# Second attention of a two-layer program: mask and row maximum in one VectorE instruction

## The reference, cut to what matters

```python
keys    = einsum('bse,neh->bsnh', residual, W_key) + Bias_key
queries = einsum('bse,neh->bsnh', residual, W_query) + Bias_query
values  = einsum('bse,neh->bsnh', residual, W_values) + Bias_values
scores  = einsum('bknh,bqnh->bnqk', keys, queries) / sqrt(64)
scores  = where(q_idx < k_idx, 1e-10, scores)      # causal: the future gets 1e-10, not -inf
probs   = softmax(scores, axis=3)
out     = einsum('bqnh,nhe->bqe', einsum('bnqk,bknh->bqnh', probs, values), W_output) + Bias_output
```

## Time and profile before

| | |
|---|---|
| median of 3 runs | 2212.29 us (2203.16 to 2216.28) |
| profiled execution, first to last instruction | 2208.8 us |
| PE busy | 1973.9 us, 89% |
| DVE busy | 1437.3 us, 65% |
| ACT busy | 981.3 us, 44% |
| POOL busy | 585.7 us, 27% |
| second attention, batch 0 | about 686 to 1030 us |
| second attention, batch 1 | about 1770 to 2110 us |

### The profile page before, as it was taken

How to read it: one execution, slowest core, us unless ns; L and a number is a source line. 1 busy time by engine, 2 the same in 40 slices (tenths; PEclk the granted TensorE clock), 3 DMA queues, 4 the chain that set the end, 5 groups by cost and what they waited for, 6 DMA issues and landing times.

```text
span 2208.8 us, 32078 instructions
## 1 busy us (share of the span) xinstructions
PE 1973.9 (89%) x10106; PEld 1173.6 (53%) x10106; DVE 1437.3 (65%) x2492; ACT 981.3 (44%) x1377; POOL 585.7 (27%) x549
## 2 busy tenths in 40 slices
PE   6899999996997999998888999999979889999985
PEld 4444444443784555556644444444448755555554
DVE  7677788865327777753467877778561377777343
ACT  2445454441224666662334444444413256656422
POOL 0000000000101798884120000000010047897821
PEclk7999999998887999998879999999979879999987
DMA  2366665578000000000516566656760000000024
GB/s 94 84 154 160 155 147 139 141 160 236 27 1 10 3 9 6 1 1 30 162 39 153 142 145 142 144 141 152 180 199 1 1 10 11 1 6 1 1 81 134
DMA packets 84847, 188.01 MB, mean 85 GB/s; under 512 B 17697, under 2 KB 46754, under 8 KB 83106
## 3 DMA queue, kind: packets, MB, share of 16 engines
q1 hardware_dynamic: 83650, 183.76, 32.9%
q0 software_dynamic: 1024, 2.10, 0.3%
HBM read 178.47 MB, written 8.91 MB: 85 GB/s over the span
## 4 chain that ended last, share of the span: by engine, by line
PE 67%; DVE 14%; issue 9%; ACT 3%; DMA 3%; POOL 3%; SPq 1%; DVEq 0%; another core or an unknown queue 0%; POOLq 0%; ACTq 0%
PE PS L814 10%; PE PS L786 5%; PE PS L750 5%; PE PS L986 4%; PE PS L926 4%; PE PS L966 3%; DVE mx L1919 3%; PE PS L881 3%; PE PS L1159 3%; PE PS L969 3%; PE PS L771 3%; PE PS L776 3%; PE PS L1218 2%; DMA V<-weight_rows 2%; POOL Esum L2463 2%
## 5 line engine op out<-in xcount | busy, mean ns | idle before, releaser
L1919 DVE TENSOR_REDUCE mx<-PS 128x8 f32<-128x512 f32 x512 | 329.5, 685 | 178.7 <-PE PS L750 163.9
L2463 POOL TENSOR_TENSOR Esum<-Esum,EE 128x512 f32<-128x512 f32 (+3 forms) x320 | 340.2, 1092 | 15.2 <-POOL Esum L2463 10.7
L1948 DVE TENSOR_TENSOR EE<-EE,V 128x1024 f32<-128x1024 f32 x256 | 303.0, 1218 | 46.2 <-DMA V<-weight_rows 45.8
L1502 ACT ACTIVATE EE<-PS 128x1024 f32<-128x1024 f32 x256 | 260.1, 1025 | 142.5 <-PE PS L776 140.5
L2052 DVE TENSOR_REDUCE mrow<-PS 128x1 f32<-128x512 f32 (+3 forms) x384 | 204.8, 552 | 98.5 <-PE PS L929 70.3
L2405 POOL TENSOR_TENSOR QA<-hT,QA 128x512 fp32r<-128x512 f32 x2 | 2.6, 1284 | 996.8 <-ACT hT L1690 996.8
L814 PE MATMUL PS<-EE,Vlater 128*64 128x512 f32 x1024 | 250.7, 609 | 9.4 <-ACT U L1468 8.3
L750 PE MATMUL PS<-KA,QA 128*128 128x512 f32 x512 | 204.1, 454 | 31.9 <-DVE mx L1919 25.9
L1586 ACT ACTIVATE EE<-PS 128x1024 f32<-128x1024 f32 (+2 forms) x192 | 138.2, 740 | 120.2 <-PE PS L969 118.1
L771 PE MATMUL PS<-QA,KA 128*128 128x512 f32 x512 | 185.1, 443 | 0.0
L750 PEld LDWEIGHTS PS<-KA,QA 128*128 128x128 f32 x512 | 97.8, 196 | 130.5 <-DVE mx L1919 88.5
(11 more groups left out here) (321 smaller groups left out, 3386.1 us busy)
## 6 DMA issues: line engine op xcount, KB each, us to landing
V<-weight_rows SPq DMA_DIRECT2D x512, 256.0 KB, 5.5
EE<-in_w SPq DMA_DIRECT2D x48, 192.0 KB, 2.7
V<-in_Wg SPq DMA_DIRECT2D x4, 1024.0 KB, 6.4
EE<-in_Wu SPq DMA_DIRECT2D x4, 1024.0 KB, 11.4
EE<-in_Wd SPq DMA_DIRECT2D x4, 1024.0 KB, 13.2
sorted_out<-U SPq DMA_DIRECT2D x12, 256.0 KB, 3.3
wo<-in_wo SPq DMA_DIRECT2D x5, 512.0 KB, 4.4
wq_s<-in_wq SPq DMA_DIRECT2D x17, 128.0 KB, 3.0
```

The lines of the kernel that those rows point to most:

```text
L1502: act.activation(EE[i % 2][:, t, :], banks(2 * (t % 2)), ACT.Exp, scale=QSCALE).then_inc(s["p2_exp"], 1)
L1919: dve.tensor_reduce(mx[:, t, half * 8:half * 8 + 8], banks(5 + x % 2, BANK).rearrange("p (c k) -> p c k", c=8), AX, ALU.max).then_inc(s["p ...
L1948: dve.tensor_tensor(EE[i % 2][:, t, :], EE[i % 2][:, t, :], weight_ring[a % 2][:, odd, :], ALU.mult).then_inc(p3_mul, 1)
L2463: ins = pool.tensor_tensor(Esum[:, h, lo:hi], Esum[:, h, lo:hi], e_tile(t)[:, h, lo - t * P:hi - t * P], ALU.add)
```

## The change

DVE's reduction of a unit becomes a `tensor_tensor_reduce`: it adds a bf16 mask operand to the PSUM columns, writes the sum to a scratch tile (`seT`), and takes the maximum of the row and of a starting value that is read per partition. For an own unit the mask is a slice of a new tile `causal` (512 zeros, then `neg`) that ends in `neg`; for the others it is 512 zeros. The starting value is the floor `eps_row` in the first half, and the first half's maximum (`mhalf1`) in the second, so that the own unit's result goes straight into `mx1`. PE's mask product goes, and so do `top` and the semaphores `m_both` and `m_top`; `turn_maxima` waits for `mx_red` instead. A semaphore increment (`s_held`) stands between each unit's wait and its instruction.

```diff
-        ident_b = sb("ident_b", [P, P], BF16)
-        neg_b = sb("neg_b", [P, P], BF16)
+        causal = sb("causal", [P, BANK + P], BF16)
...
-        mrow1 = sb("mrow1", [P, 2, NT, 2])
-        mtop1 = sb("mtop1", [P, 2, NT])
+        mhalf1 = sb("mhalf1", [P, 2, NT // 2])
...
@@ PE, maxima
-                        own = hi == (t + 1) * P
-                        mm = pe.matmul(banks(4 + h, hi - lo), M1[h][p % 2][:, t * P:(t + 1) * P],
-                                       S1[h][p % 2][:, lo:hi], start=True, stop=not own)
-                        if own:
-                            mm = pe.matmul(banks(4 + h, P, hi - lo - P), ident_b[:, :], neg_b[:, :],
-                                           start=False, stop=True)
-                        mm.then_inc(s["mx_full"], 1)
+                        pe.matmul(banks(4 + h, hi - lo), M1[h][p % 2][:, t * P:(t + 1) * P],
+                                  S1[h][p % 2][:, lo:hi], start=True, stop=True).then_inc(s["mx_full"], 1)
...
@@ PE, turn_maxima
-                    pe.wait_ge(s["m_top"], n0 + p + 1)
+                    pe.wait_ge(s["mx_red"], (n0 + p + 1) * NU)
...
@@ PE, in front of project_qk(p + 2, 1) and project_qk(1, 1)
-                        pe.wait_ge(s["mx_red"], (n + 2) * NU)
-                pe.wait_ge(s["mx_red"], (n0 + 1) * NU)
...
@@ DVE, maxima
+                        own = (t + 1) * P == half * BANK + width
+                        floor = const("eps_row")[:, t:t + 1]
+                        if half:
+                            floor = mhalf1[:, h, t - NT // 2:t - NT // 2 + 1]
                         dve.wait_ge(s["mx_full"], n * NU + x + 1)
-                        dve.tensor_reduce(mrow1[:, h, t, half:half + 1], banks(4 + h, width), AX,
-                                          ALU.max).then_inc(s["mx_red"], 1)
-
-                def top(p):
-                    n = n0 + p
-                    dve.wait_ge(s["mx_red"], (n + 1) * NU)
-                    dve.tensor_reduce(mtop1[:, :, :], mrow1[:, :, :, :], AX, ALU.max).then_inc(s["m_both"], 1)
-                    dve.wait_ge(s["m_both"], n + 1)
-                    dve.tensor_tensor(mx1[:, :, 0:33:32].rearrange("p t h -> p h t"), mtop1[:, :, :], const("eps_row").unsqueeze(1).to_broadcast([P, 2, NT]),
-                                      ALU.max).then_inc(s["m_top"], 1)
+                        dve.sem_inc(s_held, 1)
+                        mask = causal[:, BANK + P - width:BANK + P] if own else causal[:, 0:BANK]
+                        dve.tensor_tensor_reduce(seT[:, h * BANK:h * BANK + width], banks(4 + h, width), mask, 1.0, floor, ALU.add, ALU.max,
+                                                 mx1[:, t, 32 * h:32 * h + 1] if own else
+                                                 mhalf1[:, h, t - NT // 2:t - NT // 2 + 1]).then_inc(s["mx_red"], 1)
...
@@ DVE, pair and the opening
-                        top(p + 1)
-                top(0)
...
@@ DVE, once at the start
-            dve.memset(mrow1[:, :, :, :], -3e38)
+            dve.memset(causal[:, 0:BANK], 0.0)
-            dve.tensor_copy(ident_b[:, :], ident)
-            dve.tensor_copy(neg_b[:, :], const("neg"))
+            dve.tensor_copy(causal[:, BANK:BANK + P], const("neg"))
```

More of the change, by code:

```diff
@@ L350, in layer_program @@
                                                 "mt_ps m_rows p2_full p2_exp u_full u_out").split()})
-        S[1].update({n: sem(f"{n}_1") for n in ("proj_qk hi_out lo_out proj_v v_out mx_full mx_red m_both m_top mt_ps "
+        S[1].update({n: sem(f"{n}_1") for n in ("proj_qk hi_out lo_out proj_v v_out mx_full mx_red  mt_ps "
                                                 "m_row_a m_row_b f_ps f_exp p2_full p2_exp diag val_done masked later "
@@ L2131, in pair @@
                     if follows:
-                        top(p + 1)
-                    if follows:
                         row_a(p + 1)
```

## The result

| | before | after |
|---|---|---|
| median of 4 runs each, taken together | 2209.81 us (2203.16 to 2216.28) | 2231.72 us (2229.82 to 2240.26) |
| ratio | | 1.0113 (95%: 1.0092 to 1.0134) |
| profiled execution, span | 2208.8 us | 2227.7 us |
| both second attentions, from their start to that of the experts | 723.8 us | 747.9 us |

The change costs 1.1%, 21.9 us. The forecast was 2208.0, with 2231 as its upper end.

What follows compares the result with a forecast made beforehand. Steady pairs were taken as PE-bound from unit 2 to 18, then DVE-bound until the transposes. At d = 0.12, twelve turns gave -6.7 us and two openings +2.4: 2212.3 - 4.3 = 2208.0 us, full range 2192 to 2231.

Steps and rivals of the forecast that it cites:

- step 1: Pair's start, units 0 and 1 to unit 2's product: mask -0.07, lag +0.10, plus d; together +0.03 + d us.
- step 3: From unit 8 to unit 18: five mask products gone from PE, -0.35 us; DVE's start on unit 18 moves -0.40 + 3d.
- lag: Increment between wait and instruction starts DVE +0.10 us later wherever it waits for PE, nothing where busy; ends 0 and 0.10.
- steps 1 and 2: Pair's start to unit 8: masks save PE 0.07 by unit 2, 0.28 by unit 5; unit 8 shifts -0.15 + 3d us.
- d: Time the fused instruction adds per unit on DVE: 0.12 us, with ends 0.06 and 0.25.
- Step 5: Pair's end, between unit 23's reduction and PE's transposes: `top` gone, -1.24 us a turn.
- Steps 4 and 5: Pair's end: units 18 to 23 on a busy DVE add 6d; then `top` gone gives -1.24 us.
- The opening: Start of a batch, PE and DVE alternating on two banks: 13d - 0.34, +1.2 us per batch at d = 0.12.
- DVE as the bound: Rival: at units 18 to 23, d = 0.25 costs 1.5 us against `top`'s 1.24; about 2225 us, chance 0.20.
- A free maximum: Rival: d up to 0.08, DVE's last stretch hardly grows and `top` is won in full; about 2200 us, chance 0.26.
- POOL holding up the fused instruction: Rival: each unit suffers 0.5 us beside busy POOL, d = 0.62; about 2262 us, chance 0.06.
- Freed PE time arriving: Rival: the hold-up at unit 8 dissolves, a pair shrinking by at most 2.11 us; 2187 us, chance 0.05.

Runs made afterwards that it cites:

- a_fill: Kernel after plus ten products nobody reads in PE's two waits at a pair's start (six before unit 0, four between units 1 and 2): 2210.42 us, ratio 1.0006.
- b_no_mask: Kernel before without PE's mask products, maxima taken over unmasked blocks: 2207.61 us, ratio 1.0001.
- b_no_top: Kernel before without `top`, the own unit's maximum going straight to the transposes: 2200.50 us, ratio 0.9963.
- b_fused_only: Kernel before with the fused instruction (mask of zeros) and its increment in place of the reduction, mask products and `top` kept: 2216.19 us, ratio 1.0041.
- a_fill_late: Kernel after plus ten filling products in mid-pair before the value projection, in six pairs of a batch: 2250.11 us, ratio 1.0194.
- a_early: Kernel after with unit 0 taken ahead of the wait for the second head's queries: 2204.75 us, ratio 0.9978.
- b_early: Kernel before with unit 0 taken ahead of the wait for the second head's queries, nothing else changed: 2194.30 us, ratio 0.9943.

## Why the prediction was wrong

**The step that failed** is in no term of the sum: "From unit 2 to unit 18 the chain runs through PE, product after product" was costed with PE's products as long as before. Every step held the granted clock at 1.00 and took unit 0's place behind the turn as fixed. Both moved. Unit 0 came 0.6 us later, the hop to unit 2 grew by step 1's own +0.15, and the clock fell in six of the ten turns in which it had stood at 1.00. Those six falls cost 12.7 us against the kernel's own turns without one; a_fill, with nothing changed but the waits filled, gains 21 us by the medians, first turns and last pairs included. The forecast looked at PE's wait at the end of a pair and valued it in time only.

Not every wait of that size does it. Before's own turn has PE idle for 1.15 us with the clock at 1.00, as this slice of before shows (columns as in the earlier trace rows):

```profile
822.00:824.00 2.00, 1.01 (x9) 1.04 (x10) 0.89 (x1) 0.16 (x1) 2.00 (x2) 1.00 0.00 0
```

The Trainium skill (TensorE: Matmul & The Clock Gate, A second HAM failure mode: psum-queue depth-cycling) says that an engine which idles briefly and often between groups of products can swing between its two clock levels. The runs agree: no wait of PE between the turn at 778.2 and the fall at 786.1 is over 0.86 us, and filling the waits ends the falls in the second to sixth turns.

**Point by point, at full clock.** Turn 2 of batch 0 is the clean place: the clock holds there in all the kernels of the table, and unit 0 starts 7.17 to 7.18 behind the turn.

| per turn, us | forecast | turn 2 | steady turn | from |
|---|---|---|---|---|
| mask products gone (step 3) | -0.35 | -0.34 | -0.35 | b_no_mask |
| `top` gone | -1.24 | -1.17 | -0.75 | b_no_top |
| fused instruction and lag, with the masks of steps 1 and 2 | +1.03 (9d - 0.05) | +0.41 net | +0.38 net | b_fused_only |
| all of it | -0.56 | -0.55 | +0.05 | after |

- The sum. In turn 2 it came out, -0.55 against -0.56. In a steady turn unit 0 is 0.62 later (7.91 against 7.29) and the turn 0.60 worse than in turn 2. So even with the clock at 1.00 throughout, the forecast's 6.7 us over twelve turns would have been about nothing; a_fill, whose clock holds, is level with before.
- That agreement in turn 2 is in part luck. The last `diagonal` of that pair took 0.57 (at 774.87) instead of 1.20, a gain that stands in no step. If all of it came through, the fused instructions cost about 0.6 more than the 1.03 forecast; b_fused_only, taken with its own relief, says 1.25. For the same reason the three parts of turn 2 don't add up to the whole: each meets POOL in other places.
- Masks (steps 2 and 3): right in size.
- d = 0.12: measured 0.14 where somebody waits, 0.07 on a busy DVE. The read of the accumulator is a second instruction, as the Trainium skill (VectorE: DVE Perf Modes, Two Vector instructions with no wait between them) says; 384 reads of 82 ns agree. That it runs beside the next instruction was not in the forecast.
- The lag: the fused unit 0 starts at 786.36 behind a product that ends at 786.17, 0.19 against the 0.04 of a plain reduction (792.46 behind a mask that ends at 792.42). +0.15, not +0.10.
- Step 5 (`top`, -1.24): right where unit 0 keeps its place, -1.17. What its removal moves against POOL was not asked.
- Steps 4 and 5 both take DVE's last unit as what releases the transposes, with 0.3 to 0.6 us of PE's wait left. In after it isn't. DVE's last read ends at 819.87, and PE goes from its own products straight into the transposes 0.41 us later:

```profile
819.79 0.08 DVE L2049 DVE_READ_ACCUMULATOR2_ANT mx<- 128x1 f32 x1
820.16 0.28 PE L962 MATMUL PS<-QD,KD 65*128 65x128 f32 x1
820.28 1.04 PE L931 MATMUL PS<-consts,mx 128*33 128x128 f32 x8
```

The wait of 1.15 is gone whole in all ten turns from the second on. What DVE costs PE at that pair's end is the wait for unit 20, ahead of unit 22's product, 0.69 us against 0.26 in before.
- The last turn of a batch: right. From `denominators` of pair 5 to those of pair 6 it takes 33.9 us before and 34.2 after, and between 33.7 and 34.2 in every experiment but one stretch of a_fill_late.
- The opening: right. From unit 0's reduction to the first transposes it took 18.96 us (686.28 to 705.24) and now takes 20.27 (678.31 to 698.58), +1.3 against +1.2.
- The start of the kernel at zero: nothing in these runs speaks against it, and none measures it.

**The rivals.** DVE as the bound gave the nearest time, 2225, for a reason that didn't hold: it wanted d over 0.18, and PE waiting for DVE's last units. A free maximum: no. POOL holding up the fused instruction: no, 744 ns in the mean at 512 columns. But POOL does hold up `diagonal`, in other places than before, which is how part of the loss begins. Freed PE time arriving beyond the sum's 0.35: no, b_no_mask gives just that.

**What stays open.** When exactly the clock falls. With unit 0 at 7.69 it fell twice or three times, at 7.28 never in before and b_fused_only, but three times in b_no_mask, and twice in a_early at 6.89. In b_no_mask they begin at the turn itself, where PE has waited for `top`. Turns of one kernel that look alike differ in it. That `diagonal` meets POOL's sums is read from the timelines, and no run moved the one against the other. The fused instruction without the increment in front of it wasn't tried.

## What to carry to other kernels

On a chain that runs through PE, write down what each edit does to PE's waits as well as to its work, and look at the granted clock turn by turn: a few tenths of a us more waiting at the head of a stage cost 1% here, and a needed product moved into the wait (b_early) gave 0.6%. A short instruction taken out of one engine's list shifts that list against the others; name what it will now run beside. Where PE must wait and no needed work can be moved there, a product that nobody reads can be worth its place, but only in the wait (a_fill against a_fill_late).

## What the runs showed of the hardware that was not expected

- The granted clock fell to 0.50 for 3.4 to 10.2 us at a time in pairs of which PE was busy 93%. The longest fall of after began behind one wait of 0.86 us, the others in the second to sixth turns behind two, of 0.84 to 0.86 and 0.49 to 0.84 us; ten bf16 products in those waits, 1.4 us of PE's time, kept it at 1.00.
- The accumulator's read (82 ns) starts together with the next instruction on DVE, so a `tensor_tensor_reduce` of 512 columns costs 0.07 us over a plain reduction when DVE is busy and 0.14 when the result is waited for.
- A `COPY_PREDICATED` of 128x256 took 0.45 us when it began in a pause of POOL's, and 1.07 when it began inside one of POOL's additions.
